# Reordering TensorE's step by tiling mode in a two-block Swin kernel on one core

## The chip, the cores and the metric

The kernel runs on one core of one Trainium2 chip. The metric is the device time of one execution in microseconds, the lower the better. The engines are TensorE (PE in the profile; PEld is its weight load), VectorE (DVE), ScalarE (ACT), GpSimd (POOL) and SyncE (SP), which issues the DMAs.

## The reference

Input: 32 images of 192 channels and 32 x 32 pixels, float32. Two Swin transformer blocks follow each other:

```python
x = _L0_conv_ref(x, ...)   # shifted windows, relative position bias, mask
x = _L1_conv_ref(x, ...)   # shifted windows, no bias, no mask
# each block, per token (C = 192, 12 heads of 16, windows of 8 x 8, shift 4):
h   = layernorm(x) * g1 + b1;  roll by -4, split into windows of 64 tokens
q, k, v = h @ w_qkv + b_qkv
p   = softmax(q @ k.T * 16 ** -0.5 (+ bias[head] + mask))
x   = x + roll((p @ v) @ w_proj + b_proj)
h   = layernorm(x) * g2 + b2
x   = x + gelu(h @ w_fc1 + b_fc1) @ w_fc2 + b_fc2      # 192 -> 768 -> 192
```

## The kernel before, in words

**Tiles, groups and steps.** A tile is two windows, 128 tokens. An image has 8 tiles, a group is 4 tiles of one image and one layer, and there are 32 x 2 x 8 = 512 visits of tiles in 128 groups; groups of layer 1 of one image alternate with groups of layer 0 of a later one. All engines run the same loop `run(slot)` over steps `s`, each with its own hand-written order of the work for several tiles at once (tile `s` is at its scores, tile `s + 3` at its q and k product, and so on). Semaphores count what is done; `ge(name, n)` waits until `name` is done for tile `n`, and `landed(...)` waits for a transfer.

**Precision.** Most products are done in fp16 with a high and a low part (three products instead of one, or five blocks of 128 rows for 192 channels), so most values have a "hi" and a "lo" instruction. One engine makes the high part, another the low part, and a DMA transposition by SP brings both into the layout that TensorE contracts over.

**A tile's way.** `x_transpose` (layer 0, tile s+6), statistics, `mean_variance` and `centre` on VectorE, `scale`, `apply1` and `norm1_lo` on GpSimd, `norm1_turn` (DMA), `qk_product` (s+3), `qk_hi` on ScalarE, `qk_lo` on VectorE, `qk_turn` (DMA), then in step s `v_product`, `scores`, `row_max` on VectorE, `shift_scores` (subtracts the maxima by matmul), `exp` on ScalarE; in the next step `p_transpose`, `p_hi`, `p_lo` and `pv_product`; then `inverse_sums` and `o_norm` on VectorE, `o_hi` and `o_lo` on GpSimd, `o_turn` (DMA), `projection` (tile s-3), `attention_residual`, and the second norm (`centre` treats tile m's first norm and tile m-8's second together), `apply2`, `norm2_hi`, `norm2_lo`, `norm2_turn` (DMA).

**The MLP** works on a whole group in a phase of four steps, places 0 to 3 of `mlp_phase(s)`. In place 0 TensorE issues `hidden(0)` to `hidden(2)`, P.V, and `hidden(3)`; in place 1 `hidden(4)` and `hidden(5)` first. Each is five matmuls of 512 columns into one half of `ps_s`, the PSUM tile that also holds the scores; `hidden(0)` waits for `exp`, and each from `hidden(2)` on waits for the gelu two back. `gelu(m)` on ScalarE (L694) writes one of two buffers, `hidden_hi` on GpSimd (L1101) and `hidden_lo` on VectorE (L934) split it, and `gelu(m)` waits for `hidden_lo(m-2)`. `mlp_out` (L584, 18 matmuls and a bias) runs once in place 1, twice in place 2 and once in place 3; the first waits for `hidden_lo(5)`. Before the gelus ScalarE loads the gelu table, after them the exp table.

**TensorE's order** in step s: the hidden blocks of place 1; x_transpose; projection (L451, L453); v (L484); bias matmuls (L500, layer 0) and scores (L509); P's transposition (L529); y_transpose; mlp_out in place 2; shift (L518); q and k (L451, L453); hidden blocks or mlp_out; P.V (L546). Of these v and P.V use TensorE as 128x64 tiles, the scores as 64x64, everything else the whole array; the profile shows it as `128*64` and `64*64` ahead of the shapes.

Of the kernel before, what the change touches and what calls it, by code (L numbers as in the profile page):

```python
# [38 lines left out]
F16 = mybir.dt.float16  # L39
# [14 lines left out]
GROUP = 4  # L54
# [14 lines left out]
XT, QK = 6, 3  # L69
# [38 lines left out]
def mlp_phase(s):  # L108

    return (s - 7) // GROUP, (s - 7) % GROUP  # L110
# [28 lines left out]
def swin_program(nc, x, layers, rel_bias, ident_in, q_mask_in, k_mask_in, out):  # L139
    H2 = C // 2  # L140
    with ExitStack() as ctx:
# [56 lines left out]
        xt = sb("xt", [128, XT, 3, TOK], F16)  # L198
        ht = sb("ht", [128, 2, 3, GROUP * TOK], F16)
# [34 lines left out]
        LANDED = {name: [sem(f"{name}{r}") for r in range(4)] for name in ("xt_in", "ht_in", "ot_in", "qkt_in")}  # L234
# [28 lines left out]
        def run(slot):  # L263

            for s in range(-6, TOTAL + GROUP + 9):
                slot(s)
# [14 lines left out]
        def _(sp):  # L281
# [68 lines left out]
            def slot(s):  # L350
# [4 lines left out]
                def norm1_turn(n):  # L355

                    ge("lo1", n)
                    ge("v_mm", n - XT)
                    sp.dma_start_transpose(xt[:, n % XT], xs[:, 0, n % 2].rearrange("p a c -> p (a c)"))\  # L359
                        .then_inc(LANDED["xt_in"][n % 4], 16)  # L360

                def norm2_turn(n):

                    ge("lo2", n)
                    ge("fc1", (n // GROUP - 2) * HC + HC - 1)
                    tok = slice((n % GROUP) * TOK, (n % GROUP + 1) * TOK)
                    sp.dma_start_transpose(ht[:, n // GROUP % 2, :, tok], xs[:, 1, n % 2].rearrange("p a c -> p (a c)"))\  # L367
                        .then_inc(LANDED["ht_in"][n % 4], 16)
# [27 lines left out]
                for n, places in ((s - 9, (0, 1)), (s - 13, (2, 3))):  # L396
# [13 lines left out]
        def _(pe):  # L410
# [28 lines left out]
            def slot(s):  # L439
# [26 lines left out]
                def qk_product(n):  # L466
# [4 lines left out]
                    landed(pe, "xt_in", n)  # L471
                    contract(ps_qk[:, 0:2 * C], w_qkv[layer], xt[:, n % XT], 0, 2 * C, b_qk[layer][:, :])\
                        .then_inc(S["qk_mm"], 1)

                def v_product(n):
# [5 lines left out]
                    for w in range(2):  # L481
                        for i, (blk, part) in enumerate(((0, 0), (0, 3), (2, 2), (1, 1), (1, 4))):
                            for par in range(2):
                                last = mm(ps_v[par * 64:par * 64 + 64, w * H2:(w + 1) * H2].rearrange("p (g d) -> p g d", d=HD),  # L484
                                          xt[:, n % XT, blk, w * WIN:(w + 1) * WIN],
# [4 lines left out]
                def scores(n):  # L490

# [5 lines left out]
                    landed(pe, "qkt_in", n)  # L497
# [4 lines left out]
                    else:  # L502
# [684 lines left out]
```

## Time and profile before

| | |
|---|---|
| time, median of 3 runs | 4575.76 us (4570.68 to 4579.37) |
| profiled execution, first to last instruction (its span and own time) | 4581.9 us |
| busy: TensorE, VectorE, GpSimd, ScalarE | 91%, 74%, 66%, 61% |
| TensorE's granted clock, mean | 0.997 |
| the core's DMA engines, mean busy share | 51% |

Busy shares are of the span. A matmul's end is modelled from its start, and consecutive matmuls overlap, so a busy time of a block (first start to last end) is longer than its distance to the next block's start by up to one matmul. The idle time in brackets, and in the waits, is counted from such an end.

### The profile page before, as it was taken

The page shows a single profiled execution, that of the slowest core. Times are in us where ns is not written, and L with a number is a line of the kernel's source. Part 1 is how long each engine was busy: PE and PEld are TensorE (multiplying, and loading weights), DVE is VectorE, ACT ScalarE, POOL GpSimd, SP SyncE. Part 2 cuts the span into 40 slices and gives each one's busy share as a digit, 9 for nine tenths or more (in the row PEclk, how much of TensorE's full clock was granted, in tenths as well). Part 3 has the DMA queues.
Part 4 walks back from the last instruction along what each step waited for, and adds up shares of the span by engine and source line. Part 5 has one row for each costly group of instructions (what it writes and reads, how often), then busy time and mean ns, then how long its engine had stood idle before and what let it go on. Part 6 is the DMA issues. An engine that isn't in the chain of part 4 may idle for free.

```text
span 4581.9 us, 175946 instructions
## 1 busy us (share of the span) xinstructions
PE 4184.2 (91%) x66384; PEld 2968.4 (65%) x66384; DVE 3378.2 (74%) x9085; ACT 2779.7 (61%) x5921; POOL 3009.4 (66%) x6257
## 2 busy tenths in 40 slices
PE   4899999999999999999999999999999999999998
PEld 2666666666666666666666666666666666666665
DVE  6777777777777777777777777777777777777775
ACT  1566666666666566666666666666666666666665
POOL 4666666666666666666666666666666666666664
PEclk9999999999999999999999999999999999999999
DMA  4455545454545455555555555455555555545453
GB/s 101 89 90 96 88 93 97 90 94 92 96 88 96 90 93 92 94 93 92 94 94 91 92 93 96 87 93 94 95 91 94 93 92 93 96 92 92 87 90 60
DMA packets 1560581, 420.60 MB, mean 92 GB/s; under 512 B 1457462, under 2 KB 1558202, under 8 KB 1559740
## 3 DMA queue, kind: packets, MB, share of 16 engines
q1 hardware_dynamic: 1559740, 409.35, 50.4%
q8 instruction: 532, 8.72, 0.8%
q14 instruction: 309, 2.53, 0.2%
HBM read 31.56 MB, written 25.17 MB: 12 GB/s over the span
## 4 chain that ended last, share of the span: by engine, by line
PE 44%; SPq 17%; DVE 11%; POOL 10%; issue 8%; DMA 7%; ACT 2%; DVEq 0%; POOLq 0%; ACTq 0%
PE ps_s L572 13%; PE bank L584 9%; DMA ht<-xs 6%; SPq L359 6%; PE bank L451 6%; PE bank L546 5%; POOL hid L1101 5%; DVE smax L896 4%; DVE hid L934 3%; SPq L367 3%; SPq L382 3%; SPq L374 2%; PE bank L484 2%; POOL xs L1094 2%; ACT scaled L694 2%
## 5 line engine op out<-in xcount | busy, mean ns | idle before, releaser
L934 DVE TENSOR_TENSOR hid<-scaled,hid 128x512 f16<-128x512 f32 x768 | 600.5, 782 | 587.0 <-POOL hid L1101 565.5
L572 PE MATMUL ps_s<-ht,w_fc 128*128 128x512 f16 x3840 | 879.9, 382 | 127.0 <-DMA ht<-xs 125.4
L1039 POOL TENSOR_TENSOR rstd<-vare,half 128x2 f32<-128x2 f32 x520 | 361.5, 695 | 956.2 <-DVE vare L874 956.2
L584 PE MATMUL bank<-w_fc,hid 128*128 128x192 f16 x9216 | 845.9, 246 | 8.0 <-DVE hid L934 5.6
L584 PEld LDWEIGHTS bank<-w_fc,hid 128*128 128x128 f16 x9216 | 769.0, 98 | 78.5 <-issue 50.8
L1101 POOL TENSOR_SCALAR hid<-scaled 128x512 f16<-128x512 f32 x768 | 564.5, 735 | 366.4 <-ACT scaled L694 365.6
L694 ACT ACTIVATE scaled<-ps_s,b_fc 128x512 f32<-128x512 f32 x768 | 529.6, 690 | 415.1 <-PE ps_s L572 245.0
L572 PEld LDWEIGHTS ps_s<-ht,w_fc 128*128 128x128 f16 x3840 | 357.6, 98 | 576.8 <-issue 183.8
L896 DVE TENSOR_REDUCE smax<-ps_s 128x12 bf16<-128x768 f32 x512 | 488.2, 954 | 131.3 <-PE ps_s L509 107.6
L686 ACT ACTIVATE pt<-ps_t 128x768 f16<-128x768 f32 x512 | 415.2, 811 | 257.6 <-PE ps_t L529 254.6
L675 ACT ACTIVATE v_blk<-bank 64x192 f16<-64x192 f32 x1024 | 335.0, 327 | 305.2 <-PE bank L484 298.5
L451 PE MATMUL bank<-w_qkv,xt 128*128 128x384 f16 x2560 | 500.9, 326 | 6.2 <-DMA xt<-xs 3.6
L901 DVE TENSOR_TENSOR pt<-ps_t,pt 128x768 f16<-128x768 f32 x512 | 489.5, 956 | 13.4 <-issue 1.5
L659 ACT ACTIVATE xs<-xn 128x192 f16<-128x192 f32 x512 | 184.9, 361 | 518.0 <-POOL xn L1045 518.0
L680 ACT ACTIVATE stage<-ps_s 128x768 f32<-128x768 f32 x512 | 417.3, 815 | 131.7 <-PE ps_s L518 131.6
L666 ACT ACTIVATE qk<-bank 128x384 f16<-128x384 f32 x1024 | 448.2, 495 | 45.2 <-PE bank L453 43.4
L529 PE MATMUL ps_t<-ident,stage 128*128 128x128 f32 x3072 | 447.3, 282 | 0.0
L880 DVE SCALAR_TENSOR_TENSOR qk<-bank,qk 128x192 f16<-128x192 f32 x1024 | 316.5, 351 | 145.2 <-ACT qk L666 145.2
L546 PEld LDWEIGHTS bank<-v_blk,pt 128*64 128x64 f16 x18432 | 332.9, 112 | 121.2 <-issue 121.2
L518 PE MATMUL ps_s<-smax,neg_ident 128*128 128x384 bf16 x1024 | 255.0, 331 | 150.5 <-DVE smax L896 147.1
L546 PE MATMUL bank<-v_blk,pt 128*64 128x34 f16 x18432 | 383.5, 185 | 5.3 <-DVE pt L901 5.0
L890 DVE SCALAR_TENSOR_TENSOR v_blk<-bank,v_blk 64x192 f16<-64x192 f32 x1024 | 361.5, 353 | 6.8
(113 smaller groups left out, 7274.2 us busy)
## 6 DMA issues: line engine op xcount, KB each, us to landing
x_img<-in_x_dram SPq DMA_DIRECT2D x256, 96.0 KB, 2.2
out_dram<-y_img SPq DMA_DIRECT2D x256, 96.0 KB, 1.9
xt<-xs SPq DMA_TRANSPOSE x512, 2.8
qkt<-qk SPq DMA_TRANSPOSE x512, 4.0
ot<-os SPq DMA_TRANSPOSE x512, 2.3
ht<-xs SPq DMA_TRANSPOSE x512, 2.4
stage<-in_L_conv_fc_w_dram SPq DMA_DIRECT2D x2, 384.0 KB, 4.3
stage<-in_L_conv_w_fc_dram SPq DMA_DIRECT2D x2, 384.0 KB, 4.3
```

Source lines behind the costliest of these rows:

```text
L451: last = mm(dst, blocks[:, blk, :], w[:, part, n0:n1], start=(i == 0), stop=(i == 4 and bias is None))
L529: last = nc.tensor.transpose(ps_t[:, g // 3, (g % 3) * TOK:(g % 3 + 1) * TOK], p_tok[:, n % 2, g].rearrange("p a k -> p (a k)"), ident[:, :])
L546: last = mm(ps_o[rows, g * 2 * VW:(g + 1) * 2 * VW].rearrange("p (a d) -> p a d", a=2), pt[:, n % 2, ps, g, rows], v_blk[:, n % 2, vs, :, ...
L572: last = mm(ps_s[:, u % 2, :], w_fc1[layer][:, part, m * 128:(m + 1) * 128], ht[:, p % 2, blk, :], start=(i == 0), stop=(i == 4))
L584: mm(bank[:, 0:C], hid16[:, hs, m, tok], w_fc2[layer][:, ws, m, :], start=(m == 0 and i == 0), stop=False)
L666: last = copy(qk[:, n % QK, i * HEADS:(i + 1) * HEADS, places, :], src.broadcast_to([128, HEADS, 2, HD]), ACT.Copy, scale=UNSCALE)
L680: nc.scalar.activation(p_tok[:, n % 2].rearrange("p g a k -> p a g k"), ps_s[:, :, 0:PAIRS * WIN].rearrange("p a (g k) -> p a g k", g=PAIR ...
L694: nc.scalar.activation(hid[:, u % 2, :], ps_s[:, u % 2, :], ACT.Gelu, bias=b_fc1[layer][:, m:m + 1], scale=UNSCALE).then_inc(S["gelu"], 1)
L896: v.tensor_reduce(smax[:, n % 2], ps_s[:, :, 0:PAIRS * WIN].rearrange("p a (g k) -> p a g k", g=PAIRS), AX.X, ALU.max).then_inc(S["max_don ...
L901: v.tensor_tensor(pt[:, n % 2, 1].rearrange("p (b g) t -> p b (g t)", b=2), ps_t[:, :, 0:3 * TOK], pt[:, n % 2, 0].rearrange("p (b g) t -> ...
L934: v.tensor_tensor(hid16[:, 1, m, :], hid[:, u % 2, :], hid16[:, 0, m, :], ALU.subtract)\
L1101: g_.tensor_scalar(hid16[:, 0, m, :], hid[:, u % 2, :], 1.0, 0.0, ALU.mult, ALU.add)\
```

## The change

- **TensorE's order** becomes: hidden blocks of place 1; x_transpose; the bias matmuls, split off as `rel_scores` (in place 1 they stay behind v, for they wait for the last gelu); P.V of tile s-2 (it was tile s-1, at the end of the step); v; scores; projection; P's transposition; the rest as before. The six hidden blocks so have nothing between them.
- **MLP a step later:** `LATE` is 8 where 7 stood, so place 0 comes a step later for each group, and its output's transposition and stores follow; the loop has one more step.
- **Norms share a transposition:** the two norms' parts lie side by side in `xs`, and one DMA transposes the first norm of tile n and the second of tile n-8 into the ring `xh` of 8; `xt` and `ht` go. The hidden blocks read four tiles of that ring.
- **VectorE's order:** `mean_variance` of the first norm goes to the head of the step, `row_max` ahead of the attention residual and its statistics, `hidden_lo(4)` behind `inverse_sums`.
- **GpSimd's order:** `o_hi` and `o_lo` go behind the mask and `hidden_hi(5)`.

```diff
-XT, QK = 6, 3
+QK = 3
+AHEAD = 8
+LATE = 8
...
-    return (s - 7) // GROUP, (s - 7) % GROUP
+    return (s - LATE) // GROUP, (s - LATE) % GROUP
...
-        xt = sb("xt", [128, XT, 3, TOK], F16)
-        ht = sb("ht", [128, 2, 3, GROUP * TOK], F16)
+        xh = sb("xh", [128, AHEAD, 2, 3, TOK], F16)
...
-                def norm1_turn(n):
-
-                    ge("lo1", n)
-                    ge("v_mm", n - XT)
-                    sp.dma_start_transpose(xt[:, n % XT], xs[:, 0, n % 2].rearrange("p a c -> p (a c)"))\
-                        .then_inc(LANDED["xt_in"][n % 4], 16)
-
-                def norm2_turn(n):
-
-                    ge("lo2", n)
-                    ge("fc1", (n // GROUP - 2) * HC + HC - 1)
-                    tok = slice((n % GROUP) * TOK, (n % GROUP + 1) * TOK)
-                    sp.dma_start_transpose(ht[:, n // GROUP % 2, :, tok], xs[:, 1, n % 2].rearrange("p a c -> p (a c)"))\
-                        .then_inc(LANDED["ht_in"][n % 4], 16)
+                def norms_turn(n):
+
+                    first, second = live(n), live(n - AHEAD)
+                    if first:
+                        ge("lo1", n)
+                        ge("v_mm", n - AHEAD)
+                    if second:
+                        ge("lo2", n - AHEAD)
+                        ge("fc1", (n // GROUP - 4) * HC + HC - 1)
+                    which = slice(0 if first else 1, 2 if second else 1)
+                    sp.dma_start_transpose(xh[:, n % AHEAD, which].rearrange("p w b t -> p (w b) t"),
+                                           xs[:, n % 2, which].rearrange("p w a c -> p (w a c)"))\
+                        .then_inc(LANDED["xh_in"][n % 4], 16)
...
-                if live(s + 5):
-                    norm1_turn(s + 5)
-                if live(s - 3):
-                    norm2_turn(s - 3)
+                if live(s + 5) or live(s + 5 - AHEAD):
+                    norms_turn(s + 5)
...
-                def scores(n):
-
+                def rel_scores(n):
 
                     _, layer, t = visit(n)
                     if place == 1:
                         ge("gelu", p * HC + HC - 1)
                     ge("exp_done", n - 1)
-                    landed(pe, "qkt_in", n)
                     if layer == 0:
                         for par in range(2):
                             mm(ps_s[:, par, 0:PAIRS * WIN], pair_ident[:, :], bias_tab[:, par, :, :],
                                start=True, stop=False, skip_group_check=True)
-                    else:
+
+                def scores(n):
+
+                    _, layer, t = visit(n)
+                    landed(pe, "qkt_in", n)
+                    if layer == 1:
...
-                    if mlp and place == 2:
+                    if mlp and place == 3:
...
-                            landed(pe, "ht_in", n)
+                            landed(pe, "xh_in", n + AHEAD)
                         ge("exp_done", min(s, ENDS))
                     if m >= 2:
                         ge("gelu", u - 2)
                     for i, (part, blk) in enumerate(((0, 0), (3, 0), (2, 2), (1, 1), (4, 1))):
-                        last = mm(ps_s[:, u % 2, :], w_fc1[layer][:, part, m * 128:(m + 1) * 128],
-                                  ht[:, p % 2, blk, :], start=(i == 0), stop=(i == 4))
+                        last = mm(ps_s[:, u % 2, :].rearrange("p (a t) -> p a t", a=GROUP),
+                                  w_fc1[layer][:, part, m * 128:(m + 1) * 128],
+                                  xh[:, p % 2 * GROUP:(p % 2 + 1) * GROUP, 1, blk, :], start=(i == 0), stop=(i == 4))
...
+                if live(s) and place != 1:
+                    rel_scores(s)
+                if live(s - 2):
+                    pv_product(s - 2)
+                if live(s):
+                    v_product(s)
+                if live(s) and place == 1:
+                    rel_scores(s)
+                if live(s):
+                    scores(s)
                 if live(s - 3):
                     projection(s - 3)
-                if live(s):
-                    v_product(s)
-                    scores(s)
                 if live(s - 1):
                     p_transpose(s - 1)
-                if place == 1 and live(s - 9) and visit(s - 9)[1] == 1:
-                    y_transpose(s - 9)
+                if place == 1 and live(s - LATE - 2) and visit(s - LATE - 2)[1] == 1:
+                    y_transpose(s - LATE - 2)
...
-                if live(s - 1):
-                    pv_product(s - 1)
...
-                    landed(act, "ht_in", n - 2)
-                    copy(xs[:, 1, n % 2, 0, :], xn[:, 1, n % 2, :], ACT.Copy).then_inc(S["hi2"], 1)
+                    landed(act, "xh_in", n - 2 + AHEAD if n > 1 else -1)
+                    copy(xs[:, n % 2, 1, 0, :], xn[:, 1, n % 2, :], ACT.Copy).then_inc(S["hi2"], 1)
...
+                if mlp and place == 1:
+                    hidden_lo(2)
+                    hidden_lo(3)
+                if live(s + 5):
+                    mean_variance(s + 5, 0)
                 if live(s - 2):
                     inverse_sums(s - 2)
                 if mlp and place == 1:
-                    hidden_lo(2)
+                    hidden_lo(4)
                 if live(s - 2):
                     o_norm(s - 2)
-                if mlp and place == 1:
-                    hidden_lo(3)
-                    hidden_lo(4)
+                if live(s):
+                    row_max(s)
                 if live(s - 3):
                     attention_residual(s - 3)
                     statistics(s - 3, 1)
                 if live(s):
-                    row_max(s)
                     v_lo(s)
                 if mlp and place == 1:
                     hidden_lo(5)
-                if live(s + 5):
-                    mean_variance(s + 5, 0)
...
                     hidden_hi(4)
                 if live(s - 4):
                     norm2_lo(s - 4)
-                if live(s - 2):
-                    o_hi(s - 2)
-                    o_lo(s - 2)
                 if live(s + 3):
                     set_mask(s + 3)
                 if mlp and place == 1:
                     hidden_hi(5)
+                if live(s - 2):
+                    o_hi(s - 2)
+                    o_lo(s - 2)
                 if live(s + 10) and visit(s + 10)[1] == 0 and s + 10 >= TILES:
                     order_next(s + 10)
```

## Rows read from the trace of the kernel before

**Rows 1.** The page of the profile: its first line.

```profile
span 4581.9 us, 175946 instructions
```

**Rows 2.** One source line: the hidden layer's matmuls; count, ns min/median/max, first and last start.

```profile
L572 PE MATMUL ps_s<-ht,w_fc x3840: 376/379/634, 141.1 to 4561.9; 128*128 128x512 f16 x192
```

**Rows 3.** TensorE's timeline, 2003 to 2008 us: start, us, line, operation, count.

```profile
2003.21 0.75 PE L546 MATMUL bank<-v_blk,pt 128*64 128x34 f16 x36
2003.89 0.59 PE L451 MATMUL bank<-w_proj,ot 128*128 128x192 f16 x5
2004.31 0.25 PE L453 MATMUL bank<-b_out,bias_rows 128*128 128x192 f16 x1
2004.49 0.62 PE L484 MATMUL bank<-w_qkv,xt 128*64 128x96 f16 x20
2005.04 0.50 PE L500 MATMUL ps_s<-bias_tab,pair_ident 128*128 128x384 f16 x2
2005.46 0.38 PE L509 MATMUL ps_s<-qkt 64*64 64x64 f16 x24
2005.78 0.87 PE L529 MATMUL ps_t<-ident,stage 128*128 128x128 f32 x6
2006.49 1.65 PE L584 MATMUL bank<-w_fc,hid 128*128 128x192 f16 x18
```

**Rows 4.** Timeline of all engines, 2020 to 2027 us; in brackets the idle time before.

```profile
2020.72 0.88 PE L529 MATMUL ps_t<-ident,stage 128*128 128x128 f32 x6
...
2021.63 0.81 ACT L686 ACTIVATE pt<-ps_t 128x768 f16<-128x768 f32 x1 [0.88 <-PE ps_t L529]
...
2021.87 0.50 PE L518 MATMUL ps_s<-smax,neg_ident 128*128 128x384 bf16 x2 [0.27 <-DVE smax L896]
...
2022.21 0.97 PE L451 MATMUL bank<-w_qkv,xt 128*128 128x384 f16 x5
2022.40 0.81 ACT L680 ACTIVATE stage<-ps_s 128x768 f32<-128x768 f32 x1
...
2023.02 0.33 PE L453 MATMUL bank<-b_qk,bias_rows 128*128 128x384 f16 x1
...
2025.08 0.51 POOL L1045 TENSOR_SCALAR xn<-x_mid,nmean,rstd 128x192 f32<-128x192 f32 x1
...
2025.65 3.40 PE L572 MATMUL ps_s<-ht,w_fc 128*128 128x512 f16 x15 [2.31 <-DMA ht<-xs]
```

**Rows 5.** Waits: total us, times, longest.

```profile
PE ps_s L518 <- DVE smax L896: 147.1, 324, 1.1
...
PE ps_s L572 <- DMA ht<-xs: 125.4, 111, 4.8
...
PE bank L451 <- DMA ot<-os: 19.6, 36, 1.2
...
PE ps_s L500 <- ACT scaled L694: 12.7, 61, 0.5
```

**Rows 6.** Groups by line: busy us, mean ns of one, idle before and its releaser.

```profile
L934 DVE TENSOR_TENSOR hid<-scaled,hid 128x512 f16<-128x512 f32 x768 | 600.5, 782 | 587.0 <-POOL hid L1101 565.5 <-ACT scaled L694 4.5
L1101 POOL TENSOR_SCALAR hid<-scaled 128x512 f16<-128x512 f32 x768 | 564.5, 735 | 366.4 <-ACT scaled L694 365.6 <-issue 0.2
L694 ACT ACTIVATE scaled<-ps_s,b_fc 128x512 f32<-128x512 f32 x768 | 529.6, 690 | 415.1 <-PE ps_s L572 245.0 <-DVE hid L934 152.3
...
L546 PE MATMUL bank<-v_blk,pt 128*64 128x34 f16 x18432 | 383.5, 185 | 5.3 <-DVE pt L901 5.0
...
L484 PE MATMUL bank<-w_qkv,xt 128*64 128x96 f16 x10240 | 315.7, 209 | 0.0
...
L854 DVE BATCH_NORM_STATS2 bn<-x_tok 128x6 f32<-128x192 f32 x512 | 182.3, 356 | 8.8
L921 DVE SCALAR_TENSOR_TENSOR x_tok<-bank,x_tok 128x192 f32<-128x192 f32 x512 | 181.8, 355 | 99.1 <-PE bank L586 75.3 <-PE bank L453 14.7
```

**Rows 7.** Transfers: line, engine, operation, count, us to landing.

```profile
qkt<-qk SPq DMA_TRANSPOSE x512, 4.0
```

More of the change, by code:

```diff
@@ L233, in swin_program @@
         S = {name: sem(name) for name in COUNT}
-        LANDED = {name: [sem(f"{name}{r}") for r in range(4)] for name in ("xt_in", "ht_in", "ot_in", "qkt_in")}
+        LANDED = {name: [sem(f"{name}{r}") for r in range(4)] for name in ("xh_in", "ot_in", "qkt_in")}
         x_loaded = [sem(f"x_loaded{h}") for h in range(2 * SLABS)]
@@ L263, in run @@
         def run(slot):
-            for s in range(-6, TOTAL + GROUP + 9):
+            for s in range(-6, TOTAL + GROUP + 10):
                 slot(s)
@@ L395, in slot @@
                     load(visit(s + 9)[0] + 1, visit(s + 9)[2])
-                for n, places in ((s - 9, (0, 1)), (s - 13, (2, 3))):
+                for n, places in ((s - LATE - 2, (0, 1)), (s - LATE - 6, (2, 3))):
                     if live(n) and visit(n)[1] == 1 and n % GROUP in places:
@@ L470, in qk_product @@
                     ge("resid1", n - 6)
-                    landed(pe, "xt_in", n)
-                    contract(ps_qk[:, 0:2 * C], w_qkv[layer], xt[:, n % XT], 0, 2 * C, b_qk[layer][:, :])\
+                    landed(pe, "xh_in", n)
+                    contract(ps_qk[:, 0:2 * C], w_qkv[layer], xh[:, n % AHEAD, 0], 0, 2 * C, b_qk[layer][:, :])\
                         .then_inc(S["qk_mm"], 1)
@@ L737, in slot @@
                     p_hi(s - 1)
-                if place == 1 and live(s - 9) and visit(s - 9)[1] == 1:
-                    y_evac(s - 9)
+                if place == 1 and live(s - LATE - 2) and visit(s - LATE - 2)[1] == 1:
+                    y_evac(s - LATE - 2)
                 if last_block and place == 2:
@@ L1058, in apply1 @@
                     ge("lo1", n - 2)
-                    landed(pool, "xt_in", n - 2)
+                    landed(pool, "xh_in", n - 2)
                     pool.nop(nofuse=True)
-                    normalise(n, 0, xs[:, 0, n % 2, 0, :], "hi1")
+                    normalise(n, 0, xs[:, n % 2, 0, 0, :], "hi1")
                     normalise(n, 0, xn[:, 0, n % 2, :], "ln1")
@@ L1078, in norm2_lo @@
                     ge("hi2", n)
-                    g_.tensor_tensor(xs[:, 1, n % 2, 1, :], xn[:, 1, n % 2, :], xs[:, 1, n % 2, 0, :],
+                    g_.tensor_tensor(xs[:, n % 2, 1, 1, :], xn[:, 1, n % 2, :], xs[:, n % 2, 1, 0, :],
                                      ALU.subtract).then_inc(S["lo2"], 1)
@@ L1093, in norm1_lo @@
                     ge("hi1", n)
-                    g_.tensor_tensor(xs[:, 0, n % 2, 1, :], xn[:, 0, n % 2, :], xs[:, 0, n % 2, 0, :],
+                    g_.tensor_tensor(xs[:, n % 2, 0, 1, :], xn[:, 0, n % 2, :], xs[:, n % 2, 0, 0, :],
                                      ALU.subtract).then_inc(S["lo1"], 1)
```

2 lines of the change are left out of this document (1 added, 1 removed).

## The prediction

> **What bounds the kernel now.** I read the page first (its span), then the hidden layer's line, TensorE's own timeline of a whole step, the timeline of all engines where the hidden layer starts, the waits, and last the mean durations by line and the transfers. The reader is to see four things.
>
> First, the loop is long and regular: 128 groups of four steps in a span of 4581.9. The first hidden matmul starts at 141.1 us and the last at 4561.9 [rows 1, 2]; taking off some 8 us for the stage that the last one ends, 127 periods are (4420.8 - 8) / 127 = 34.75 us. A tenth of a microsecond in each group is 12.8 us in the whole.
>
> Second, TensorE sets the pace in most places, for its blocks follow one another with no gap [rows 3], and part of that time is no arithmetic. Five projection matmuls of 192 columns take 2003.89 to 2004.31, 0.084 each, but from the sixth (L453) to the 64-column-wide v product is 0.18: **0.10 us is lost on entering** the other tiling mode. The P.V block is busy 0.75 and one of its matmuls lasts 0.185 [rows 6], so its 36th starts at +0.565, 0.016 apart, and the next block at +0.68: 0.10 lost on leaving. The v block by the same working (20 matmuls, 0.62 busy, 0.21 each, next block at +0.55) loses 0.12 on leaving. The two bias matmuls L500 need 0.42 until the 64x64 scores start, while two like them (L518 to L451, 0.34) need less when no mode changes [rows 4]: 0.08. The scores leave their mode for L529; that can't be read alone, and I take the v block's 0.12. A step of layer 0 so pays 0.10 + 0.10 + 0.10 + 0.12 + 0.08 + 0.12 = 0.62, a step of layer 1 (no bias matmuls) 0.53.
>
> Third, there are two real waits [rows 5]. The shift matmuls L518 wait for the row maxima, 147.1 us in 324 waits. The idle column undercounts, since ends are modelled: L529 to L584 takes 0.71 unhindered [rows 3], L529 to L518 takes 1.15 [rows 4], a stall of 0.44 where the view has 0.27. With 0.17 more for each it is 202 us, 1.6 a group. The hidden layer L572 waits for the transposed norm, 125.4 us in 111 waits, plus 0.16 each by the same reading (2023.02 to 2025.65, less L453's 0.16, is 2.47 where the view has 2.31): 143 us, 1.1 a group.
>
> Fourth, the hidden stage has a second limit behind TensorE. One hidden block of 5 matmuls is 1.08 us (15 busy for 3.40, the last one 0.38 long [rows 2, 4], so 14 steps of 0.216), but its result goes through gelu 0.69, the fp16 part on GpSimd 0.735 and the rest on VectorE 0.782 [rows 6] in two buffers: with some 0.25 of hand-overs 2.45 us for two blocks, 1.23 each. Today P.V stands in the middle of the stage, and the wait for the transposition ahead of it.
>
> **The change, part by part.**
>
> *Order by tiling mode.* Bias, P.V, v, scores, projection leave one entry (0.10), v to scores (0.12) and scores to projection (0.12): 0.34. Layer 0 saves 0.28 a step, layer 1 0.19, and the place-1 step of layer 0, where the bias stays behind v, 0.19. A group saves 3 x 0.28 + 0.19 = 1.03 or 4 x 0.19 = 0.76; mean 0.90. No row shows P.V followed by v. Its cost lies between nothing and another 0.10 a step (0.4 a group); both carry the form 128*64 in the rows [rows 3], so I take nothing. The Trainium skill (TensorEngine Tiling (Array Packing), Tiling Modes, Key Properties) says that changing the mode drains the engine and changing only the tile does not. By that the 0.90 stands whole; if a tile change cost as much as a mode change it would be 0.5.
>
> *Projection behind the scores.* It puts 0.50 us (6 x 0.084) of TensorE's work between scores and shift. Call E the start of the block behind the scores. Today the shift starts right behind the maxima, at E+1.15 (E is 2020.72, [rows 4]); it is now reached at E + 0.50 + 0.71 = E+1.21. The wait of 1.6 a group goes, except in place 1, where VectorE has hidden_lo(4) and the normalisation of O ahead of the maxima; I keep 0.25 there.
>
> *But exp moves with it.* ScalarE copies P out (0.81) ahead of exp (0.81) [rows 4]. P's copy started 0.91 after L529; now at E+1.41, so exp ends at E+1.41 + 0.77 + 0.81 = E+2.99. The first hidden block must wait for exp, as it overwrites the scores, and TensorE is there at E + 1.21 + 0.34 + 0.98 = E+2.53. New wait in place 0: **0.5**.
>
> *MLP a step later, norms sharing a transposition.* The last tile's norm now lands a step (8 us) ahead of need; the 1.1 goes. SP issues one transposition in place of two; the one four times as large as either old one (qkt) lands in 4.0 us [rows 7], less than the slack, so the merged one is hidden. Its wait for both norms' low parts holds back on SP's queue only O's transposition and the image loads, and P.V two tiles back has put O's use a step away as well. A step's delay of the MLP adds one short slot at the tail, 1 us. Cover gone: small waits for O's transposition (19.6 us) and for gelu ahead of the bias (12.7 us) [rows 5], together 0.25 a group, go too.
>
> *The hidden stage laid bare.* Blocks 0 to 5 now stand in a row, 6.5 us, without P.V between. Count from the first, h. gelu(0) ends at about h+2.15 (1.08, a hand-over, a table load behind exp that hardly holds it back, and 0.69). GpSimd ends its normalising 3.7 us after the shift today (L1045 at 2025.08, 0.51 long, [rows 4]); VectorE now has the residual and its statistics (0.36 each, [rows 6]) between the maxima and the centring that GpSimd waits for, so it is 4.45 after the shift, h+2.6. Then hidden_hi(0) to 3.35, hidden_lo(0) to 4.2, gelu(2) to 4.95, and hidden(4), due at 4.33, starts at 5.0: **0.67** (part of it shown as hidden(3) waiting for gelu(1), behind q,k's copy). hidden_lo(1), behind q,k's low part, ends at 5.65, gelu(3) at 6.4, and hidden(5) starts at 6.45 for 6.08: 0.37. New: **1.05** a group. Bounds: 0.3 if GpSimd is free as early as now, 2.5 if each link takes a fifth longer than its mean.
>
> *VectorE's order in place 1.* From the end of the maxima, residual and statistics (0.72), v's low part (two instructions like the residual, 0.72) and hidden_lo(5) (0.78) take 2.3 with hand-overs; TensorE needs 0.34 + 0.98 = 1.32 until the MLP's second layer, which waits for hidden_lo(5). That is a wait of 0.98; today, with residual and statistics ahead of the maxima, the same sum gives 0.2 or a little less. **0.8** new, between 0.3 and 1.3.
>
> **The sum.** Gone: 0.90 + 1.6 + 1.1 + 0.25 = 3.85 a group. New: 0.25 + 0.5 + 1.05 + 0.8 = 2.6. Net 1.25 x 128 = 160 us, less 1 for the tail: 4582 - 159 = 4423 of span. The median of the runs shown, 4575.8, is 6 us below that span, so I expect **4417 us**.
>
> **Rivals.**
>
> *A. The hidden stage hides its chain.* If gelu(m-2) is always there in time and hidden_lo(5) too, 1.85 of the new waits fall away: net 3.1 x 128 = 397 us, 4180. For it: in today's rows L572 waits for gelu almost never. Against it: today P.V and the late transposition stand in that stage. Half of it gives 4300.
>
> *B. Slower: VectorE and GpSimd's chain takes over from TensorE in places 0 and 1.* The centring is late, so hidden_hi(0) is, and each link takes a fifth above its mean: 2.85 us for two blocks, 0.35 a block over TensorE's 1.08 for the four behind the first pair, which is 1.4, on top of the 0.8 by which GpSimd is late for the first pair, and 0.5 if it is later still. The stage's wait is then 2.7 and not 1.05, and place 1 adds the upper 1.3: 2.15 more than my sum, 0.9 us a group worse than now, 4690. It decides from 1.25 us a group above my new waits, that is from a stage wait of 2.3. For it: VectorE's hidden_lo already waits 565.5 us for GpSimd [rows 6], 4.4 a group, so every delay of GpSimd goes straight into the chain. Against: in places 2 and 3 TensorE has the second layer's 18 matmuls (1.65 busy, [rows 3]) ahead of each thing it needs, and the others catch up. The Trainium skill (TensorEngine Tiling (Array Packing), PSUM Bottleneck) warns that a faster TensorE does not evacuate PSUM faster; that is this case, and the trace bears it out so far as the 1.23 against 1.08 us a block.
>
> *C. The modes cost the same in the new order* (P.V to v pays, and the removed waits hid part of the drains): 0.4 a group less, 4468.
>
> *D. The gain is small or nil*: the stage's wait is 1.9 to 2.4 us, with 4525 to 4590.
>
> **How the numbers follow.** Forecast with C, 4350 to 4500: 0.60. A or half of it, 4180 to 4350: 0.20. D: 0.10, of which 0.03 within 0.2% (9 us, about what a measurement of this kernel can tell from no change) and 0.02 above. B: 0.10. Faster 0.85, same 0.03, slower 0.12. Leaving out the lower half of A and the upper part of B and D gives the range 4280 to 4540; the likeliest case's own is 4350 to 4500.
>
> **What would show it.** The profile after should have no idle time of L572 due to a DMA, and its waits due to ScalarE instead (exp on the first block, gelu on the 4th to 6th), some 1.5 us a group. L518's wait for the maxima should drop under 50 us. P.V must be followed by v at 36 x 0.016 with no 0.10 gap, projection by nothing of another mode. The MLP's second layer (L584) should wait for hidden_lo(5), some 0.8 a group. I am wrong if the stage of six hidden blocks takes 6.6 us (case A) or over 9 (case B), or if SP's queue, now with one large transposition, lets q,k's land late.

## The result and the profile after

The changed kernel takes **4314.1 us** (median of 4 runs, 4313.7 to 4317.5) against 4575.0 of the kernel before in the same call: a ratio of 0.9431 (95% interval 0.9418 to 0.9445), 261 us less, 2.0 us for each of the 128 groups. I had expected 4417 in a range of 4280 to 4540: right in direction, with a gain forecast 103 us or 0.8 us a group too small. 4314 also lies below the likeliest case's own 4350 to 4500, in the band of 4180 to 4350 to which I had given 0.20.

The page of the changed kernel, its first line (TensorE is busy 93% of the span, before 91%; VectorE 78%, before 74%):

```profile
span 4312.3 us, 175439 instructions
```

TensorE's timeline of the changed kernel: the step of place 0, the six hidden blocks (four at its end, two at the head of place 1), the step of place 1, and the start of place 2 (start, us, line, operation, count, idle before). L547 is P.V, L482 v, L510 the scores, L449 and L451 the projection or q and k, L530 P's transposition, L519 the shift, L573 the hidden layer, L586 the second layer, L496 the bias, L460 `x_transpose` and L595 `y_transpose`:

```profile
2001.85 0.75 PE L547 MATMUL bank<-v_blk,pt 128*64 128x34 f16 x36
2002.44 0.60 PE L482 MATMUL bank<-w_qkv,xh 128*64 128x96 f16 x20
2002.97 0.38 PE L510 MATMUL ps_s<-qkt 64*64 64x64 f16 x24
2003.28 0.59 PE L449 MATMUL bank<-w_proj,ot 128*128 128x192 f16 x5
2003.70 0.25 PE L451 MATMUL bank<-b_out,bias_rows 128*128 128x192 f16 x1
2003.79 0.82 PE L530 MATMUL ps_t<-ident,stage 128*128 128x128 f32 x6
2004.44 0.49 PE L519 MATMUL ps_s<-smax,neg_ident 128*128 128x384 bf16 x2
...
2005.58 0.33 PE L451 MATMUL bank<-b_qk,bias_rows 128*128 128x384 f16 x1
2006.30 7.17 PE L573 MATMUL ps_s<-xh,w_fc 128*128 128x512 f16 x30 [0.39 <-ACT stage L687]
2013.40 0.75 PE L547 MATMUL bank<-v_blk,pt 128*64 128x34 f16 x36
...
2015.03 0.50 PE L496 MATMUL ps_s<-bias_tab,pair_ident 128*128 128x384 f16 x2 [0.44 <-ACT scaled L701]
...
2016.94 0.38 PE L595 MATMUL bank<-ident,x_tok 128*96 128x128 f32 x2
2017.16 0.49 PE L519 MATMUL ps_s<-smax,neg_ident 128*128 128x384 bf16 x2
...
2019.03 1.65 PE L586 MATMUL bank<-w_fc,hid 128*128 128x192 f16 x18 [0.40 <-DVE hid L941]
...
2020.59 0.33 PE L460 MATMUL bank<-ident,x_win 96*128 96x96 f32 x2
2020.76 0.49 PE L496 MATMUL ps_s<-bias_tab,pair_ident 128*128 128x384 f16 x2
```

Read it against [rows 3, 4].

- P.V to v is 0.59, which is 35 distances of 0.016 and 0.03 more: no mode change is paid between two blocks of the same mode. The Trainium skill's rule that a drain comes with a change of mode and not of tile (TensorEngine Tiling (Array Packing), Tiling Modes) holds here. From the projection's sixth matmul to P's transposition is 0.09 where 0.18 stood ahead of v.
- P's transposition takes 0.65 to the next block's start where it took 0.71 behind the 64x64 scores. I had not counted that.
- The shift follows P's transposition at once. The wait for the maxima is 0 here.
- The first hidden block starts 0.72 behind the last matmul of q and k (L451), 0.16 of which is L451 itself: 0.56 of waiting for exp.
- The stage from the first hidden block to P.V is 7.10; six blocks of 1.08 and 0.10 for the mode are 6.58: 0.52 of waiting for gelu. In the mean of all groups the fourth, fifth and sixth block start 0.12, 0.23 and 0.19 late. The waits below have only 5.2 us of this for L573, for each delay is about as short as the 0.16 that idle counting leaves out. Then 0.44 at the bias for the last gelu, and 0.40 idle at L586 for hidden_lo(5), some 0.56 with the 0.16 that idle counting leaves out.

The waits of the changed kernel (total us, times, longest), against [rows 5]:

```profile
DVE hid L941 <- POOL hid L1109: 430.7, 506, 3.3
...
ACT scaled L701 <- DVE hid L941: 306.8, 510, 1.4
...
PE bank L586 <- DVE hid L941: 71.9, 128, 2.9
...
PE ps_s L573 <- ACT stage L687: 47.6, 123, 0.4
...
PE ps_s L496 <- ACT scaled L701: 27.9, 62, 0.7
...
PE ps_s L510 <- ACT scaled L701: 24.0, 64, 0.7
...
PE ps_s L519 <- DVE smax L903: 11.5, 57, 1.1
```

The DMA is gone from L573's waits but for 1.6 us, and the maxima's 147.1 is 11.5. New or longer are the four waits on exp, gelu and hidden_lo (the bias waited 12.7 for gelu before). L941's wait for GpSimd, 565.5 in [rows 6], is 430.7. And gelu waits for the buffer that hidden_lo frees twice as long as before (152.3 in [rows 6]): that is what now paces it.

The other engines in the same change-over:

```profile
2004.64 0.81 ACT L693 ACTIVATE pt<-ps_t 128x768 f16<-128x768 f32 x1 [0.90 <-PE ps_t L530]
...
2005.35 0.80 ACT L687 ACTIVATE stage<-ps_s 128x768 f32<-128x768 f32 x1
...
2007.58 0.69 ACT L701 ACTIVATE scaled<-ps_s,b_fc 128x512 f32<-128x512 f32 x1
2007.74 0.99 POOL L1053 TENSOR_SCALAR xn<-x_tok,nmean,rstd 128x192 f32<-128x192 f32 x2
...
2008.69 0.62 POOL L1109 TENSOR_SCALAR hid<-scaled 128x512 f16<-128x512 f32 x1
...
2009.42 0.69 DVE L941 TENSOR_TENSOR hid<-scaled,hid 128x512 f16<-128x512 f32 x1 [2.23 <-POOL hid L1109]
...
2010.20 0.69 ACT L701 ACTIVATE scaled<-ps_s,b_fc 128x512 f32<-128x512 f32 x1 [0.60 <-DVE hid L941]
```

P's copy (L693) stands ahead of exp (L687), as the prediction had it. GpSimd is busy normalising (L1053) up to 2008.7, and hidden_hi(0) (L1109) starts then, 2.39 behind the first hidden block (predicted: 2.6), though gelu(0) (L701) ended at 2008.27. From there the chain ran faster than the prediction's means: hidden_hi(0) took 0.62 and hidden_lo(0) (L941) 0.69, so that gelu(2) started 3.90 behind the first block where 4.2 was forecast.

### The profile page after: what moved, and what is told of

It reads as the page before. It is cut to its first block and busy times, and to the rows that moved or that the text cites. A ratio compares the mean times of both kernels' runs of the same rounds, so it can differ in the third digit from the quotient of the medians.

```text
span 4312.3 us, 175439 instructions
## 1 busy us (share of the span) xinstructions
PE 4027.5 (93%) x66384; PEld 2912.2 (68%) x66384; DVE 3364.9 (78%) x9085; ACT 2709.6 (63%) x5921; POOL 3062.7 (71%) x6257
## 5 line engine op out<-in xcount | busy, mean ns | idle before, releaser
L573 PE MATMUL ps_s<-xh,w_fc 128*128 128x512 f16 x3840 | 909.7, 380 | 60.7 <-ACT stage L687 47.6
L941 DVE TENSOR_TENSOR hid<-scaled,hid 128x512 f16<-128x512 f32 x768 | 597.9, 779 | 449.7 <-POOL hid L1109 430.7
L586 PE MATMUL bank<-w_fc,hid 128*128 128x192 f16 x9216 | 847.7, 246 | 77.7 <-DVE hid L941 71.9
L586 PEld LDWEIGHTS bank<-w_fc,hid 128*128 128x128 f16 x9216 | 764.6, 98 | 156.7 <-DVE v_blk L897 80.6
L573 PEld LDWEIGHTS ps_s<-xh,w_fc 128*128 128x128 f16 x3840 | 335.3, 97 | 621.0 <-ACT scaled L701 217.5
L1109 POOL TENSOR_SCALAR hid<-scaled 128x512 f16<-128x512 f32 x768 | 609.4, 794 | 182.8 <-ACT scaled L701 182.2
L701 ACT ACTIVATE scaled<-ps_s,b_fc 128x512 f32<-128x512 f32 x768 | 529.3, 690 | 308.9 <-DVE hid L941 306.8
L693 ACT ACTIVATE pt<-ps_t 128x768 f16<-128x768 f32 x512 | 415.3, 811 | 324.0 <-PE ps_t L530 316.8
L449 PE MATMUL bank<-w_qkv,xh 128*128 128x384 f16 x2560 | 500.9, 326 | 6.2 <-DMA xh<-xs 3.6
L687 ACT ACTIVATE stage<-ps_s 128x768 f32<-128x768 f32 x512 | 416.0, 812 | 139.2 <-PE ps_s L519 139.2
L530 PE MATMUL ps_t<-ident,stage 128*128 128x128 f32 x3072 | 419.8, 273 | 5.1 <-issue 5.1
L547 PEld LDWEIGHTS bank<-v_blk,pt 128*64 128x64 f16 x18432 | 333.0, 112 | 128.1 <-issue 95.3
L547 PE MATMUL bank<-v_blk,pt 128*64 128x34 f16 x18432 | 383.5, 185 | 4.3 <-DVE pt L908 4.1
L449 PEld LDWEIGHTS bank<-w_qkv,xh 128*128 128x128 f16 x2560 | 245.7, 97 | 179.2 <-DVE x_mid L928 7.1
```

Of the source, the lines that this page charges most:

```text
L449: last = mm(dst, blocks[:, blk, :], w[:, part, n0:n1], start=(i == 0), stop=(i == 4 and bias is None))
L530: last = nc.tensor.transpose(ps_t[:, g // 3, (g % 3) * TOK:(g % 3 + 1) * TOK], p_tok[:, n % 2, g].rearrange("p a k -> p (a k)"), ident[:, :])
L547: last = mm(ps_o[rows, g * 2 * VW:(g + 1) * 2 * VW].rearrange("p (a d) -> p a d", a=2), pt[:, n % 2, ps, g, rows], v_blk[:, n % 2, vs, :, ...
L573: last = mm(ps_s[:, u % 2, :].rearrange("p (a t) -> p a t", a=GROUP), w_fc1[layer][:, part, m * 128:(m + 1) * 128], xh[:, p % 2 * GROUP:(p ...
L586: mm(bank[:, 0:C], hid16[:, hs, m, tok], w_fc2[layer][:, ws, m, :], start=(m == 0 and i == 0), stop=False)
L687: nc.scalar.activation(p_tok[:, n % 2].rearrange("p g a k -> p a g k"), ps_s[:, :, 0:PAIRS * WIN].rearrange("p a (g k) -> p a g k", g=PAIR ...
```

## The experiments

All were timed beside the kernel before. "Changed" is 4314 us, ratio 0.9431.

### Parts of the changed kernel undone

**Bias between P.V and v.**

```diff
-                if live(s) and place != 1:
-                    rel_scores(s)
                 if live(s - 2):
                     pv_product(s - 2)
+                if live(s) and place != 1:
+                    rel_scores(s)
```

> The changed kernel with the bias matmuls between P.V and v in every step but place 1, nothing else moved. Theory (a change of tiling mode costs TensorE about 0.10 us on entering and 0.10 us on leaving the 64-column blocks, and this is paid in full wherever TensorE has no wait behind it): 192 steps of layer 0 gain one leaving and one entering, 0.19 us each, 37 us in all, less what the waits of places 0 and 1 swallow (one step in three of these, so a third of it at most): 25 to 37 us slower than the changed kernel, 4339 to 4351. Rival (drains are hidden behind other engines' chains, the order by mode is worth nothing): within 8 us of 4314.

Measured: 4373.3 us, ratio 0.9562 (0.9544 to 0.9580), 59 us slower than changed. The rival is out; the theory's size of 25 to 37 us is too small. TensorE's timeline of this kernel, start and length first:

```profile
2001.12 0.33 PE L460 MATMUL bank<-ident,x_win 96*128 96x96 f32 x2
2001.38 0.75 PE L547 MATMUL bank<-v_blk,pt 128*64 128x34 f16 x36
2002.06 0.50 PE L496 MATMUL ps_s<-bias_tab,pair_ident 128*128 128x384 f16 x2
2002.49 0.62 PE L482 MATMUL bank<-w_qkv,xh 128*64 128x96 f16 x20
2003.04 0.38 PE L510 MATMUL ps_s<-qkt 64*64 64x64 f16 x24
```

From x_transpose (L460) to P.V is 0.26 where x_transpose to bias took 0.17 (2020.59 to 2020.76 above); P.V, bias and v take 0.68 + 0.43 + 0.55 = 1.66 to the scores, against 0.42 + 0.59 + 0.53 = 1.54. That is 0.21 a step, in 192 steps 40 us, a little above what was expected. The other 19 us are spread: from block start to block start, no line of TensorE has more than 7 us of them. What they wait for was not traced.

**Projection first.**

```diff
+                if live(s - 3):
+                    projection(s - 3)
                 if live(s) and place != 1:
                     rel_scores(s)
...
                     scores(s)
-                if live(s - 3):
-                    projection(s - 3)
```

> The changed kernel with the projection ahead of the bias, where it stood before. The number of mode changes stays, but P's transposition again follows the 64x64 scores. Theory (the projection is what covers the row maxima): the shift matmuls wait again about 0.4 us in place 3 and in place 0, more in place 1, nothing in place 2, 1.3 to 1.6 us a group; the wait of the first hidden block for exp falls from 0.55 to 0.2, and P's transposition takes 0.71 us in place of 0.655. Net 0.9 to 1.3 us a group, 115 to 165 us slower than the changed kernel: 4430 to 4480. Rival (the whole gain is the order by mode and the later MLP, the maxima's wait only moves on to exp): at most 30 us slower, under 4345.

Measured: 4567.6 us, ratio 0.9985 (0.9974 to 0.9996). One block in another place costs 253 us, nearly the whole gain. I had expected 115 to 165; the waits of this kernel:

```profile
PE ps_s L573 <- ACT scaled L701: 108.5, 127, 1.1
...
PEld bank L449 <- DVE qk L887: 103.4, 201, 2.0
PE ps_s L519 <- DVE smax L903: 92.0, 265, 1.1
```

The shift waits for the maxima again (92.0 against 11.5), as expected. What I had not expected are the other two rows. The projection shares a PSUM bank with q and k, and its weight load waits until VectorE has read it (103.4; its matmuls 30.0). In the kernel before, P.V at the end of the step stood between the two; at the head of the changed step nothing does. And the hidden blocks wait more for gelu (108.5 against 5.2).

**MLP a step earlier again.**

```diff
-LATE = 8
+LATE = 7
```

> The changed kernel with LATE = 7: the MLP's four steps a step earlier, as before, all else as changed. Theory (the transposed norm came too late, and a step more is what removed that): the first hidden block waits for the transposition again, about 1.1 us a group on average as before, of which the wait for exp (0.55 now) covers up to a half; 0.6 to 1.2 us a group, 75 to 155 us slower than the changed kernel, 4390 to 4470. Rival (sharing the transposition relieved SP's queue enough that the transfer would have been in time a step earlier too): within 25 us of 4314, with no wait of L573 for a DMA above 20 us in total.

Measured: 4401.6 us, ratio 0.9625 (0.9607 to 0.9643), 87 us slower, as the theory had it. The wait is back, in 127 of 128 groups:

```profile
PE ps_s L573 <- DMA xh<-xs: 162.4, 127, 4.7
```

**Two transpositions.**

```diff
-                    sp.dma_start_transpose(xh[:, n % AHEAD, which]..., xs[:, n % 2, which]...)
+                    for which, on, name in ((0, first, "xh_in"), (1, second, "ht_in")):
+                        if on:
+                            sp.dma_start_transpose(xh[:, n % AHEAD, which], xs[:, n % 2, which]...)
...
```

The hidden layer and `norm2_hi` wait for the second one.

> The changed kernel with the two norms transposed by two DMAs, issued one behind the other, each with its own semaphore; buffers, order and LATE as changed. Theory (with the MLP a step later nobody waits for a norm's transposition, so sharing it is worth nothing): within 10 us of 4314. Rival (SP's queue sets part of the pace, and the second issue of 1.2 to 2.6 us a step holds back O's and q,k's transpositions): 30 to 120 us slower, with waits of L449 for ot or of L510 for qkt.

Measured: 4344.8 us, ratio 0.9501 (0.9484 to 0.9518), 31 us slower. My theory falls and the rival stands. A wait of the projection for O's transposition, 0.7 us in the changed kernel and 19.6 in the kernel before, is there:

```profile
PE bank L449 <- DMA ot<-os: 37.3, 40, 2.8
```

SP's own queue fits it. Waits of SP for the first norm's low part, this kernel and then the changed one:

```profile
SPq L354 <- POOL xs L1102: 493.7, 260, 15.2
```

```profile
SPq L354 <- POOL xs L1102: 989.4, 495, 15.1
```

With one more issue a step SP waits half as much for its work, that is, it comes late to more of it, and O's transposition is issued from that same queue.

**The old order of the maxima.**

```diff
-                if live(s):
-                    row_max(s)
                 if live(s - 3):
                     attention_residual(s - 3)
                     statistics(s - 3, 1)
                 if live(s):
+                    row_max(s)
                     v_lo(s)
```

> The changed kernel with VectorE's old order of these three: attention residual, its statistics, then the row maxima; TensorE's order as changed. Theory (projection behind the scores and maxima ahead of the residual only work as a pair): the maxima start 1.2 us later against the scores in places 0, 1 and 3, of which place 0's wait for exp and place 1's wait for hidden_lo(5) give nothing back; 1.1 to 1.2 us for each, 0 to 0.7 in place 2, together 2.6 to 3.6 us a group less 0.5 that place 1 saves at the MLP's second layer: 270 to 400 us slower than the changed kernel, 4585 to 4715. Rival (VectorE's order is a side matter): under 4400.

Measured: 4584.8 us, ratio 1.0008 (0.9998 to 1.0017), 271 us slower than changed, at the theory's lower edge. The place of the maxima in VectorE's order is worth as much as the whole change. TensorE's timeline of this kernel, place 1:

```profile
2002.95 0.38 PE L595 MATMUL bank<-ident,x_tok 128*96 128x128 f32 x2
2004.16 0.50 PE L519 MATMUL ps_s<-smax,neg_ident 128*128 128x384 bf16 x2 [0.83 <-DVE smax L903]
```

y_transpose (L595) to shift is 1.21, where it is 0.22 in the changed kernel (2016.94 to 2017.16): the maxima stand behind the residual, and that behind the projection.

### Parts of the change done alone on the kernel before

**MLP a step later.** 7 becomes 8 in `mlp_phase`, the output's steps move with it (9 to 10 and 13 to 14), and the loop has one more step.

> The kernel before with the MLP's phase a step later and nothing else (orders, buffers and two transpositions as before). Theory (a step more takes the wait of the first hidden block for the transposed norm, 1.13 us a group with what exp holds of it, but gelu's table load and GpSimd's normalising then stand bare): 0.6 to 1.0 us a group, 75 to 130 us faster than before, 4445 to 4500. Rival (SP's full queue, with two transpositions of norms a step, is what makes things late, and the lateness moves to O or q,k): within 30 us of before.

Measured: 4457.2 us, ratio 0.9733 (0.9717 to 0.9749), 120 us faster: theory. Its waits:

```profile
PE ps_s L518 <- DVE smax L896: 146.7, 326, 1.1
...
PEld ps_s L572 <- DMA ht<-xs: 7.1, 19, 0.4
```

The shift's wait is what it was, 147, and the matmuls' wait for the DMA is gone (7.1 of the weight loads' is left).

**Projection behind the scores.**

```diff
-                if live(s - 3):
-                    projection(s - 3)
                 if live(s):
                     v_product(s)
                     scores(s)
+                if live(s - 3):
+                    projection(s - 3)
```

> The kernel before with the projection moved behind the scores on TensorE alone; P.V stays at the step's end, LATE and VectorE's order as before. Theory (the projection covers the maxima): of 1.65 us a group of waits of the shift 1.3 go in places 0, 2 and 3, exp takes 0.35 of it back in place 0, P's transposition behind a full-array block gains 0.055 a step, and where no x_transpose stands between P.V and v a mode change goes (0.2 in half of the steps): 1.3 to 1.7 us a group, 165 to 215 us faster than before, 4360 to 4410. Rival: VectorE's order of before has the attention residual ahead of the maxima, so the maxima now wait for the projection, and the gain is under 60 us or a loss.

Measured: 4699.0 us, ratio 1.0262 (1.0244 to 1.0281), **121 us slower**. The rival was right, with the mechanism that it named. The shift's wait for the maxima grows by 229 us, and the one for the DMA falls by 83:

```profile
PE ps_s L518 <- DVE smax L896: 376.2, 385, 1.1
...
PE ps_s L572 <- DMA ht<-xs: 42.6, 50, 4.7
```

**The same with VectorE's order.** The edit above, and on VectorE `row_max(s)` ahead of `attention_residual(s - 3)`, as in the changed kernel.

> The kernel before with two edits: the projection behind the scores on TensorE (the edit that alone made it 2.6% slower) and, on VectorE, the row maxima ahead of the attention residual and its statistics. Theory (the slower time came from the maxima standing behind the projection's residual, and with that undone the projection covers them): the shift's wait all but goes; 1.3 to 1.7 us a group faster than before, 4360 to 4410. Rival (the projection behind the scores is bad by itself, for it delays exp, the residual or the centring): no faster than before, 4560 or more.

Measured: 4645.8 us, ratio 1.0147 (1.0130 to 1.0164), 66 us slower than before. The theory falls, and the time is where the rival had it. Its waits:

```profile
PE ps_s L572 <- DMA ht<-xs: 268.9, 127, 4.7
...
PE bank L584 <- DVE hid L934: 70.7, 128, 2.9
...
PE ps_s L500 <- ACT scaled L694: 43.3, 62, 1.0
```

The shift is no longer among them: the projection does cover the maxima. But the residual comes later: in one step it starts 1.3 us behind the scores, where it started 0.9 ahead of them in the kernel before. So the second norm comes later, and the hidden layer waits 268.9 us for its transposition where it waited 125.4 [rows 5]. The second layer waits for hidden_lo(5) as in the changed kernel (71.9 there), and the bias waits longer for the last gelu (43.3 against 12.7). And the longer wait has a price of its own. TensorE's timeline of this kernel at one change-over, then the window behind the wait (us, the busy times of TensorE, its weight loads, VectorE, ScalarE and GpSimd, then the granted clock):

```profile
381.29 0.33 PE L453 MATMUL bank<-b_qk,bias_rows 128*128 128x384 f16 x1
383.94 5.08 PE L572 MATMUL ps_s<-ht,w_fc 128*128 128x512 f16 x15 [2.33 <-DMA ht<-xs]
```

```profile
384.40:387.70 3.30, 3.30 (x9) 1.16 (x8) 0.22 (x1) 1.45 (x3) 0.72 (x2) 0.50 0.74 144
```

After 2.33 us idle the granted clock is 0.50, that is 1.2 GHz, for 3.3 us of the block that follows, and 15 hidden matmuls take 5.08 where [rows 4] have 3.40. The length of the wait does not settle it: [rows 4] are at the full clock behind a wait of 2.31. In this kernel 43 of the 128 stages of hidden blocks met the half clock for more than 0.5 us, behind waits of 2.1 to 4.8 us (mean 2.9), and 85 did not, behind 1.2 to 3.1 (mean 2.0); in the kernel before 5 did. The mean clock of this execution is 0.982 (before 0.997, changed 0.999), and L572 is busy 942 us in all where it is 880 before: 62 us, about as much as the whole kernel is slower. So the move of the projection and the maxima gave nothing net here: the shift's wait turned into a wait for the norm, and that wait in part into a slower clock. It is not the later MLP alone that the pair lacks: the changed kernel with `LATE = 7` is at 4401.6, 172 us faster than before, with the other parts of the change beside the pair. Which of those parts makes the difference was not tried.

### Trying the causes of the new waits

**Statistics behind hidden_lo(5).**

```diff
                     attention_residual(s - 3)
+                if live(s - 3) and place != 1:
                     statistics(s - 3, 1)
...
                     hidden_lo(5)
+                if live(s - 3) and place == 1:
+                    statistics(s - 3, 1)
```

> The changed kernel with VectorE's second statistics of place 1 behind hidden_lo(5) in place of ahead of v's low part. Theory (the second MLP layer's first block waits 0.68 us a group for hidden_lo(5), whose way from the maxima is residual, statistics, v's low part, itself; statistics are 0.36 of that): 0.3 to 0.36 us a group, 38 to 46 us faster than the changed kernel, 4268 to 4278. Rival (the wait is given back in the next step, since centring comes no earlier and hidden_lo(5) frees nothing else): within 10 us of 4314.

Measured: 4286.9 us, ratio 0.9363 (0.9348 to 0.9378), 27 us faster than changed; expected were 38 to 46.

```profile
PE bank L586 <- DVE hid L941: 22.3, 69, 2.9
...
PE bank L547 <- DVE pt L908: 16.6, 69, 1.4
```

The second layer's wait falls by 50 us (71.9 to 22.3), more than expected, and a part is given back: P.V now waits 16.6 us (4.1 in the changed kernel) for P's low part, which VectorE makes later.

**v's low part behind the centring, in place 0.**

```diff
-                if live(s):
+                if live(s) and place:
                     v_lo(s)
...
                     centre(s + 5)
+                if live(s) and place == 0:
+                    v_lo(s)
```

> The changed kernel with v's low part of place 0 behind the centring on VectorE. Theory (the centring, and through it GpSimd's normalising, holds back hidden_hi(0) and with it the gelu chain, which makes TensorE wait 0.5 in the hidden stage and 0.5 at the scores behind it): GpSimd is free 0.7 earlier, of which hidden_hi(0) can use 0.2 to 0.4 until gelu(0) is the later one: 25 to 50 us faster, 4264 to 4289. Rival (the chain's own pace of 1.25 us a block sets the stage, not its start): within 10 us of 4314.

Measured: 4290.0 us, ratio 0.9367 (0.9348 to 0.9386), 24 us faster. The stage of this kernel is busy 6.96 where it was 7.17:

```profile
2001.89 6.96 PE L573 MATMUL ps_s<-xh,w_fc 128*128 128x512 f16 x30 [0.39 <-ACT stage L687]
```

**Both.** The last two diffs together.

> The changed kernel with both of VectorE's edits, statistics behind hidden_lo(5) in place 1 and v's low part behind the centring in place 0. The one alone gave 27 us, the other 24. They act on different waits (the MLP's second layer; the hidden stage), so if nothing is given back 51 us, 4263; rival (both feed the same cycle, GpSimd's or VectorE's, which then sets the pace): 4280 to 4290.

Measured: **4262.4 us**, ratio 0.9310 (0.9296 to 0.9324), 52 us faster than changed. The two add up; this is the fastest version here.

**P.V back in the hidden stage.** `pv_product(s - 1)` ahead of `hidden(3)` in place 0, and none in place 1.

> The changed kernel with P.V of place 0's tile s-1 back between hidden(2) and hidden(3), in place of ahead of v in place 1. Theory (the gelu chain sets the time from the first hidden block to the scores of place 1, and TensorE has 1.0 us a group of waits in it): P.V's 0.6 and a mode entry and exit of 0.2 go into waits that are there anyway: within 15 us of 4314, with hidden_hi and hidden_lo as late as before and a longer wait for the last gelu at place 1's scores. Rival (TensorE is the bound there too): 25 us slower for the two mode changes; or 50 us faster, if P.V in the stage lets gelu run ahead as it did before.

Measured: 4312.2 us, ratio 0.9424 (0.9407 to 0.9440), no difference. Its waits:

```profile
PE ps_s L496 <- ACT scaled L703: 49.8, 62, 1.1
...
PE ps_s L510 <- ACT scaled L703: 46.2, 64, 1.1
```

They are 96.0 together where the changed kernel has 51.9: P.V filled the stage's wait, and the wait came back at the scores. From the first hidden block to place 1's scores the gelu chain sets the time and not TensorE, as the theory had it.

## Why the prediction was right, and where its size was off

The direction and the range were right, and the waits that went and came are the ones forecast, but for one. The size was off by 0.8 us a group. The two traces show where, from the start of each of TensorE's blocks to the start of the next, added up over 122 groups and divided by them (us a group; the forecast's terms are put to the same stretches):

| stretch | forecast | measured |
|---|---|---|
| from P's and y's transposition to the next block (the shift, where it waited) | -1.35 | -1.68 |
| behind q and k: norm's DMA, exp, hidden_lo(5) | +0.2 | -0.06 |
| the six hidden blocks | +1.05 | +0.44 |
| behind v: last gelu | -0.1 | +0.23 |
| all the rest: changes of mode, wait for O | -1.05 | -1.01 |
| together | -1.25 | -2.08 |

- **Hidden stage** (1.05). The mechanism was right, the term was mis-sized, and it is the largest miss. TensorE waits 0.54 in the stage (0.52 in the group shown). GpSimd was released 0.2 us earlier than forecast, and I had taken 0.735 and 0.782 for hidden_hi and hidden_lo, means over all six of a group, where the first took 0.62 and 0.69. What I had not forecast at all is the wait for the last gelu behind it: I had it vanish, and it grew by 0.23. Chain and wait together so cost about 0.7 more than before, and not 0.95.
- **Order by mode** (0.90 a group). Right: the last row but one is as forecast, P.V to v costs nothing extra, and the bias experiment measured 0.21 a step for one entry and one exit on TensorE's own timeline, where 0.19 was expected. What the sum left out is P's transposition, 0.71 until the next block behind the scores and 0.655 behind a full-array block (medians over all steps), 0.22 a group.
- **Projection behind the scores** (1.6 less 0.25 for the shift). Right: the rest of the first row is 1.46 against 1.35, and the shift's wait is 11.5 us. But I treated it as a part by itself. On the kernel before it makes things 121 us worse without VectorE's order, and 66 us worse with it; in the changed kernel taking either out costs 253 and 271. That VectorE's order was in the change I had used only to count how late the centring comes, not as what the gain hangs on.
- **exp moves with it** (0.5): 0.56 in the group shown.
- **MLP a step later** (1.1): alone it gives 120 us, 0.94 a group, and taken out of the changed kernel 87.
- **VectorE's order in place 1** (0.98 in all, 0.8 of it new). Too high: 71.9 us of idle in 128 waits are 0.56, with 0.16 more each 0.7 in all. With exp's and the DMA's terms right, this is the 0.26 of the second row.
- **Sharing a transposition** (nothing). Wrong as a mechanism: undone, it costs 31 us, 0.24 a group, and what it covers is O's transposition and not a norm's. The sum hardly suffered, for it had booked the end of the wait for O (0.15) elsewhere, to P.V's new place; the experiment keeps that place, and the wait is back.

That the forecast came as near as it did is in part luck, since the terms' errors of up to 0.6 have both signs. No experiment undid P.V's move, GpSimd's order, or the new places of `mean_variance` and hidden_lo(4), so what these are worth is not shown; nor are the 19 us of the bias experiment explained.

Of the rivals, half of A (4300) is where the time came out: the gelu chain does hold TensorE back, but in the stage by half of what was forecast, and taking a part of that away by two moves on VectorE gives 4262. B, C and D are out: the links of the chain ran at means of 0.69, 0.79 and 0.78, the stage's wait was 0.5, and P.V to v costs nothing. The Trainium skill (TensorEngine Tiling (Array Packing), PSUM Bottleneck) says that tiling speeds up TensorE but not the evacuation of PSUM. The trace agrees in the one stretch between the first hidden block and place 1's scores, where TensorE waits for gelu, which reads its PSUM tile; gelu in turn waited 306.8 us for hidden_lo, so it is the chain behind the read that sets the pace. A slower kernel did come about, by a way that I had not listed: the projection's move, with or without the maxima's, on the kernel before.

## What to carry to other kernels

In a loop written out by hand for several engines, a block that is moved on one engine to cover a wait must be looked at with what its output feeds on the other engines: the same move of the projection was worth 253 us with the other parts of the change beside it, and cost 121 us alone. Group matmuls of one tiling mode: here each entry and each exit cost about 0.1 us, and where TensorE was the bound it paid them in full. When a chain on other engines sets the pace of a stretch, filling TensorE's wait there is worth nothing (4312 against 4314), and starting the chain earlier is worth something (24 us here).

## What the runs showed of the hardware

- In the version with the longest waits ahead of the hidden blocks, 43 of 128 stages ran in part at 1.2 GHz, and L572 was busy 62 us longer in all. Behind a wait of 2.33 us it was so, behind one of 2.31 in the kernel before it was not. In the changed kernel the granted clock is 1.00 from 110 to 4280 us.
- Entering or leaving the modes with 64 columns costs 0.08 to 0.12 us each ([rows 3, 4]); from one 128x64 block to the next, P.V to v, nothing beyond 0.03. The fp32 transposition of P takes 0.71 behind 64x64 matmuls and 0.65 behind full-array ones.
- One DMA transposition of twice the columns was issued in the time of one (median 1.21 us for the shared one, 1.18 for O's) and landed in a median 2.8 us against 2.5 for the halves, which took 1.25 each to issue. Sharing so saved SP's queue a whole issue of some 1.2 us a step.
